# Exponentials of the wide attention taken by ScalarE straight from the scores, one operation per head and batch

## The chip, the cores and the metric

The kernel runs on one core of one Trainium2 chip. The metric is the device time of one execution in microseconds (us). A difference of 0.2%, some 2.3 us, is about what a measurement of this kernel can tell from none.

## The reference, cut to what matters

The program is a decoder layer stack over 64 batches of 64 tokens of width 128: attention with 16 narrow heads and a cross attention, a mixture of experts, attention with 16 heads of 64 and rotary embedding, a cross attention with a padding mask and a quantised feed-forward. The change lies in the second attention alone, after a layer norm of x:

```
q, k, v = x @ Wq, x @ Wk, x @ Wv          # 16 heads of 64
q, k = apply_rope(q), apply_rope(k)
sim = einsum('bid,bjd->bij', q, k) * scale  # scale = 64 ** -0.5
sim = where(causal, sim, -inf)
attn = softmax(sim, axis=-1)
out = einsum('bij,bjd->bid', attn, v)
x = x + out @ Wo + bo
```

All of it is computed in float32; the mask is added by a small bf16 matmul.

## The kernel before, in words

Phases follow one another: narrow attention, a plan, the experts, the wide attention (`wide_attention_phase`, names with the prefix a_ in the trace), and the tail. The wide attention takes 16 blocks of 4 batches (256 tokens). A block has G = 4 steps, and a step handles one item: 4 heads of these 4 batches. An item's scores fill `S_ps`, four banks of PSUM with 128 columns each in use (2 batches side by side, 2 one above the other), and there is one `S_ps` only.

Each engine has its own instruction stream, written out by hand and ordered by semaphores; `run_blocks_farther` gives a prologue, step(0), a loop and the last three blocks. In the step of item n the engines do, in this order:

- TensorE (PE): `scores(n+1)` (8 mask matmuls, L1552, and 64 small ones, L1560), `transpose_e(n)` (L1569), the projections `project_q(n+3)`, `project_v(n+1)`, `project_k(n+3)` (L1514, L1537, L1524), in a block's first step `transpose_x` of the next block (L1503), which borrows the first bank of `S_ps`, then `project_o(n-1)` (L1596) and `weigh_values(n)` (L1584).
- VectorE (DVE): `subtract_max(n+1)`: a row maximum (L1789) and the scores less that maximum written to `E` in SBUF (L1793), the semaphore `d_ready`; `products_q(n+3)` (L1765, two instructions); `reciprocals(n+1)`: row sums of `E` (L1799) and their reciprocals (L1804); `products_k(n+3)` (L1765, two); and by the step number g in the block: `combine` of the experts' rows (g = 0 and 1, L1737), `statistics` (g = 2, L1745 to L1752), `centres` (g = 3, L1759). In g = 1 `add_residual` (L1810) stands behind `subtract_max`. The last two blocks have none of combine, statistics and centres.
- ScalarE (ACT): `evacuate_e(n)` (L1681), `exponentials(n+1)` (L1674, one instruction on `E` in place, 128x512), `evacuate_v(n+1)` (L1670), `keep_xT` or `evacuate_xT` in two of the steps, `evacuate_o(n)` (L1688), and in g = 3 `normalise` (L1645), which waits for `centres`; `slots_of` (L1695) opens g = 0.
- GpSimd (POOL): `normalise_e(n+1)` (L1440, `E` times the reciprocals), the rotations of q and k of item n+3 (L1419, L1420), a gather of expert rows (L1456).

The waits that matter: `scores(n+1)` writes `S_ps` and so waits for `d_ready` of item n. `weigh_values(n)` waits for `v_ready` of item n+1, that is for `evacuate_v(n+1)`, which stands behind `exponentials(n+1)` in ScalarE's stream. `transpose_e(n)` waits for `normalise_e(n)` and for the products of k of item n+2, with which it shares a bank.

Of the kernel before, what the change touches and what calls it, by code (L numbers as in the profile page):

```python
# [7 lines left out]
P = 128  # L8
B, T, C = 64, 64, 128
# [10 lines left out]
ALU = mybir.AluOpType  # L20
ACT = mybir.ActivationFunctionType
AX = mybir.AxisListType
# [44 lines left out]
def wait_here(eng, sem, value, passed):  # L67

    eng.wait_ge(sem, value)
    eng.sem_inc(passed, 1)  # L70
# [1220 lines left out]
def wide_attention_phase(nc, k):  # L1291
    UB = 2
# [4 lines left out]
    G = H // 4  # L1297
    GH = 4
    ITEMS = NB * G
    SCALE = float(D1) ** -0.5  # L1300
    n = "a1"
    d = k.d
    with ExitStack() as ctx:
        def sb(name, shape, dt=F32):
            return ctx.enter_context(nc.sbuf_tensor(f"{n}_{name}", shape, dt))

        def ps(name, shape):
            return ctx.enter_context(nc.psum_tensor(f"{n}_{name}_ps", shape, F32))

        def sem(name):  # L1310
            return nc.alloc_semaphore(f"{n}_{name}")
# [26 lines left out]
        row_max = sb("row_max", [P, 2, GH * UB])  # L1338
        row_sum = sb("row_sum", [P, 2, GH * UB])
        rsum = sb("rsum", [P, 2, GH * UB])  # L1340

        E = sb("E", [P, 2, GH * P])
        ET = sb("ET", [P, 2, GH * P])
# [6 lines left out]
        S_ps = ps("S", [P, GH, 512])  # L1350
# [22 lines left out]
        v_ready = sem("v_ready")  # L1373
        s_ps = sem("s_ps")
        max_ready = sem("max_ready")
        d_ready = sem("d_ready")
        sum_ready = sem("sum_ready")
        e_ready = sem("e_ready")
        rsum_ready = sem("rsum_ready")
        en_ready = sem("en_ready")  # L1380
        et_ps = sem("et_ps")
# [5 lines left out]
        passed = sem("passed")  # L1387
# [4 lines left out]
        def item_at(blk, g):  # L1392

            return blk + g // G, g % G

        def later(number, least):

            return not isinstance(number, int) or number >= least

        def at_most_all(number):  # L1400

            return min(number, ITEMS) if isinstance(number, int) else number
# [93 lines left out]
        def _(pe):  # L1496
            def transpose_x(nb):

                pe.wait_ge(xn_ready, nb + 1)
                if later(nb, 1):  # L1500
                    pe.wait_ge(d_ready, nb * G - 2)
                for u in range(UB):
                    mm = nc.tensor.transpose(S_ps[:, 0, u * P:(u + 1) * P], xn[:, u, :], k.ident[:])  # L1503
                mm.then_inc(xnT_ps, 1)
# [35 lines left out]
            def scores(blk, g):  # L1540

                n_ = blk * G + g
                pe.wait_ge(rq_ready, n_ + 1)
                if later(n_, 1):
                    pe.wait_ge(d_ready, n_)
                if g == 2:
                    pe.wait_ge(xnT_ready, min(blk + 2, NB) if isinstance(blk, int) else blk + 2)
                wait_here(pe, rk_ready, n_ + 1, passed)
                for h in range(GH):
                    half = slice(64 * (h % 2), 64 * (h % 2) + 64)  # L1550
                    for b in range(2):
                        nc.tensor.matmul(S_ps[64 * b:64 * b + 64, h, 0:P], k.causal_queries[half, 0:T], k.causal_keys[half, 0:P],  # L1552
                                         start=True, stop=False)
                for a in range(2):
                    for u in range(UB):
                        for b in range(2):
                            tok = slice((2 * b + u) * T, (2 * b + u + 1) * T)
                            for h in range(GH):
                                rows = slice(32 * h, 32 * h + 32)
                                mm = nc.tensor.matmul(S_ps[64 * b:64 * b + 64, h, u * T:(u + 1) * T], RQ[rows, g % 2, a, tok],  # L1560
                                                      RK[rows, g % 2, a, tok], start=False, stop=(a == 1 and u == UB - 1))
                mm.then_inc(s_ps, 1)
# [9 lines left out]
            def weigh_values(blk, g):  # L1572

                n_ = blk * G + g
                pe.wait_ge(et_ready, n_ + 1)
                pe.wait_ge(v_ready, at_most_all(n_ + 2))
                wait_here(pe, pq_ready, at_most_all(n_ + 4), passed)
                for j in range(2):
                    for b in range(2):
                        for u in range(UB):  # L1580
                            rows = slice(64 * u, 64 * u + 64)
                            for r in range(2):
                                h = 2 * j + r
                                mm = nc.tensor.matmul(VQ_ps[64 * r:64 * r + 64, u, j * P + b * T:j * P + (b + 1) * T],  # L1584
                                                      V[rows, g % 2, b, h * D1:(h + 1) * D1],
                                                      ET[rows, g % 2, h * P + b * T:h * P + (b + 1) * T], start=True, stop=True)
                mm.then_inc(pv_ps, 1)

            def project_o(blk, g):
                n_ = blk * G + g  # L1590
                pe.wait_ge(ot_ready, n_ + 1)
                if g == 0 and later(blk, 1):
                    pe.wait_ge(x_done, blk)
                for u in range(UB):
                    for j in range(2):
                        mm = nc.tensor.matmul(Y_ps[:, u * P:(u + 1) * P], OT[:, g % 2, u, j, :], wo[:, g, j, :],  # L1596
                                              start=(g == 0 and u == 0 and j == 0),
                                              stop=(g == G - 1 and u == UB - 1 and j == 1), skip_group_check=True)
                mm.then_inc(y_ps, 1)
# [12 lines left out]
            def step(blk, prev, nxt):  # L1612
                for g in range(G):
                    if g + 1 < G or nxt:
                        scores(*item_at(blk, g + 1))
                    transpose_e(blk, g)
                    if g + 3 < G or nxt:
                        project_q(*item_at(blk, g + 3))
                    if g + 1 < G or nxt:
                        project_v(*item_at(blk, g + 1))  # L1620
                    if g + 3 < G or nxt:
                        project_k(*item_at(blk, g + 3))
                    if nxt and g == 0:
                        transpose_x(blk + 1)
                    if g > 0:
                        project_o(blk, g - 1)
                    elif prev:
                        project_o(blk - 1, G - 1)
                    weigh_values(blk, g)

            prologue()
            step(0, prev=False, nxt=True)
            with pe.Fori(1, NB - 1) as blk:
                step(blk, prev=True, nxt=True)
            step(NB - 1, prev=True, nxt=False)
            project_o(NB - 1, G - 1)

        @block.scalar
        def _(act):
# [30 lines left out]
                nc.scalar.activation(V[:, g % 2].rearrange("p b e -> p (b e)"), V_ps, ACT.Copy).then_inc(v_ready, 1)  # L1670

            def exponentials(blk, g):
                act.wait_ge(d_ready, blk * G + g + 1)
                nc.scalar.activation(E[:, g % 2, :], E[:, g % 2, :], ACT.Exp, scale=SCALE).then_inc(e_ready, 1)  # L1674

            def evacuate_e(blk, g):
                n_ = blk * G + g
# [51 lines left out]
        def _(dve):  # L1729
# [53 lines left out]
            def subtract_max(blk, g):  # L1783

                n_ = blk * G + g
                dve.wait_ge(s_ps, n_ + 1)
                src = S_ps[:, :, 0:P].rearrange("p h (u t) -> p h u t", t=T)
                top = row_max[:, g % 2, :].rearrange("p (h u) -> p h u", u=UB)
                nc.vector.tensor_reduce(top, src, AX.X, ALU.max).then_inc(max_ready, 1)  # L1789
                if later(n_, 2):  # L1790
                    dve.wait_ge(et_ps, n_ - 1)
                dve.wait_ge(max_ready, n_ + 1)
                nc.vector.tensor_tensor(E[:, g % 2, :].rearrange("p (h u t) -> p h u t", u=UB, t=T), src,  # L1793
                                        top.unsqueeze(3).broadcast_to([P, GH, UB, T]), ALU.subtract).then_inc(d_ready, 1)

            def reciprocals(blk, g):
                n_ = blk * G + g
                dve.wait_ge(e_ready, n_ + 1)
                nc.vector.tensor_reduce(row_sum[:, g % 2, :], E[:, g % 2, :].rearrange("p (j t) -> p j t", t=T), AX.X, ALU.add)\  # L1799
                    .then_inc(sum_ready, 1)  # L1800
                if later(n_, 2):
                    dve.wait_ge(en_ready, n_ - 1)
                dve.wait_ge(sum_ready, n_ + 1)
                nc.vector.reciprocal(rsum[:, g % 2, :], row_sum[:, g % 2, :]).then_inc(rsum_ready, 1)  # L1804

            def add_residual(blk):
# [866 lines left out]
```

## Time and profile before

| what | value |
|---|---|
| three timed runs | 1155.99, 1156.0, 1155.08 us; median 1155.99 us |
| the profiled execution's own time | 1161.69 us |
| its span | 1159.9 us |
| mean granted TensorE clock | 0.898 of full speed |
| busy: PE, DVE, ACT, POOL | 997.4, 845.9, 589.2, 564.1 us |
| 800 to 900 us (wide attention): PE, DVE, ACT, POOL | 97.19, 95.57, 43.86, 86.61 us |

The profile is of one execution. Busy times are per engine and overlap; matmuls are pipelined and their ends are modelled, so a busy PE is not a PE at its peak. The wide attention runs from about 606 to 1011 us of the span.

### The profile page before, as it was taken

The page shows a single profiled execution, that of the slowest core. Times are in us where ns is not written, and L with a number is a line of the kernel's source. Part 1 is how long each engine was busy: PE and PEld are TensorE (multiplying, and loading weights), DVE is VectorE, ACT ScalarE, POOL GpSimd, SP SyncE. Part 2 cuts the span into 40 slices and gives each one's busy share as a digit, 9 for nine tenths or more (in the row PEclk, how much of TensorE's full clock was granted, in tenths as well). Part 3 has the DMA queues.
Part 4 walks back from the last instruction along what each step waited for, and adds up shares of the span by engine and source line. Part 5 has one row for each costly group of instructions (what it writes and reads, how often), then busy time and mean ns, then how long its engine had stood idle before and what let it go on. Part 6 is the DMA issues. An engine that isn't in the chain of part 4 may idle for free. (4 is left out here: it accounts for less than half of the span.)

```text
span 1159.9 us, 38655 instructions
## 1 busy us (share of the span) xinstructions
PE 997.4 (86%) x14756; PEld 801.9 (69%) x14759; DVE 845.9 (73%) x2025; ACT 589.2 (51%) x983; POOL 564.1 (49%) x705
## 2 busy tenths in 40 slices
PE   5999999999945799999947999999999999776454
PEld 2666666667642799999936888888888888654113
DVE  4878787888749244444328999999999998488576
ACT  3665656677720466666612444444444444356545
POOL 4332424353300433333226888888888887433104
PEclk9999999999955799999978999999999999856555
DMA  7200000000000111111130000000000000050002
GB/s 240 114 2 0 2 11 20 20 19 27 11 28 0 40 47 48 48 48 47 39 109 13 13 12 11 11 11 9 11 11 11 11 7 1 17 127 24 1 0 73
DMA packets 36984, 37.60 MB, mean 32 GB/s; under 512 B 7142, under 2 KB 31145, under 8 KB 36522
## 3 DMA queue, kind: packets, MB, share of 16 engines
q1 hardware_dynamic: 31690, 27.33, 7.7%
q0 software_dynamic: 4352, 8.92, 3.0%
q8 instruction: 48, 0.79, 0.3%
q10 hardware_dynamic: 866, 0.33, 0.1%
q14 instruction: 28, 0.23, 0.1%
HBM read 27.65 MB, written 8.91 MB: 32 GB/s over the span
## 5 line engine op out<-in xcount | busy, mean ns | idle before, releaser
L1283 POOL DMA_INDIRECT e_x<-xn_rows,e_where x72 | 68.4, 950 | 167.2 <-DVE e_where L1264 119.4
L360 POOL TENSOR_SCALAR n_KX<-n_KT,n_of_head 128x512 f32<-128x512 f32 x124 | 84.1, 700 | 123.1 <-ACT n_KT L601 86.3
L1253 DVE COPY e_y<-e_Y_ps 128x128 f32<-128x128 f32 x72 | 21.0, 292 | 112.4 <-PE e_Y_ps L1220 105.9
L760 DVE TENSOR_REDUCE n_row_max<-n_S_ps 128x16 f32<-128x1024 f32 x64 | 78.2, 1221 | 28.2 <-PE n_S_ps L451 28.1
L1440 POOL TENSOR_TENSOR a_E<-a_E,a_rsum 128x512 f32<-128x512 f32 x64 | 66.7, 1042 | 56.0 <-DVE a_rsum L1804 56.0
L665 ACT ACTIVATE n_ET<-n_ET_ps 128x1024 f32<-128x1024 f32 x64 | 65.5, 1024 | 46.6 <-PE n_ET_ps L461 45.8
L461 PEld LDWEIGHTS n_ET_ps<-ident,n_E 128*128 128x128 f32 x512 | 57.1, 142 | 34.9 <-issue 20.1
L764 DVE TENSOR_TENSOR n_E<-n_S_ps,n_row_max 128x1024 f32<-128x1024 f32 x64 | 78.4, 1225 | 2.9
L1210 PE MATMUL e_G_ps<-e_xT,e_gate_here 128*128 128x128 f32 x576 | 78.5, 281 | 0.9 <-ACT e_up_here L1173 0.9
L1688 ACT ACTIVATE a_OT<-a_VQ_ps 128x512 f32<-128x512 f32 x64 | 38.2, 597 | 78.4 <-PE a_VQ_ps L1584 78.4
L1220 PE MATMUL e_Y_ps<-m_down_w,e_hT 128*128 x576 | 76.7, 275 | 1.1 <-issue 0.8
L1210 PE MATMUL e_U_ps<-e_xT,e_up_here 128*128 128x128 f32 x576 | 77.6, 279 | 0.0
L461 PE MATMUL n_ET_ps<-ident,n_E 128*128 128x128 f32 x512 | 68.3, 276 | 8.1 <-ACT n_E L657 8.1
L657 ACT ACTIVATE n_E<-n_E 128x1024 f32<-128x1024 f32 x64 | 67.2, 1052 | 14.2 <-DVE n_E L764 14.2
L1210 PEld LDWEIGHTS e_G_ps<-e_xT,e_gate_here 128*128 128x128 f32 x576 | 72.3, 197 | 1.1 <-ACT e_up_here L1173 1.1
L474 PEld LDWEIGHTS n_PV_ps<-n_VB,n_ET 128*64 128x64 f32 x2048 | 65.3, 138 | 10.5 <-issue 10.5
L1184 ACT ACTIVATE e_silu<-e_G_ps 128x512 f32<-128x512 f32 x72 | 43.0, 597 | 58.3 <-PE e_G_ps L1210 48.1
L1210 PEld LDWEIGHTS e_U_ps<-e_xT,e_up_here 128*128 128x128 f32 x576 | 71.7, 196 | 0.0
L474 PE MATMUL n_PV_ps<-n_VB,n_ET 128*64 128x18 f32 x2048 | 71.7, 213 | 0.0
L1220 PEld LDWEIGHTS e_Y_ps<-m_down_w,e_hT 128*128 128x128 f32 x576 | 70.2, 192 | 1.8 <-issue 1.8
L1674 ACT ACTIVATE a_E<-a_E 128x512 f32<-128x512 f32 x64 | 40.2, 629 | 61.1 <-DVE a_E L1793 61.1
L1596 PEld LDWEIGHTS a_Y_ps<-a_wo,a_OT 128*128 128x128 f32 x512 | 66.6, 193 | 4.7 <-ACT a_OT L1688 1.2
(278 smaller groups left out, 2672.4 us busy)
## 6 DMA issues: line engine op xcount, KB each, us to landing
slot_out<-e_y SPq DMA_DIRECT2D x72, 64.0 KB
X<-in_x SPq DMA_DIRECT2D x8, 256.0 KB, 5.8
n_ctxT<-in_ctxT SPq DMA_DIRECT2D x8, 256.0 KB, 3.0
m_gate_w<-in_L_ffn_gate_w SPq DMA_DIRECT2D x1, 2048.0 KB, 7.5
m_up_w<-in_L_ffn_up_w SPq DMA_DIRECT2D x1, 2048.0 KB, 11.9
m_down_w<-in_L_ffn_down_w SPq DMA_DIRECT2D x1, 2048.0 KB, 17.7
xn_rows<-n_xn SPq DMA_DIRECT2D x8, 256.0 KB
t_ctxT<-in_ctxT SPq DMA_DIRECT2D x8, 256.0 KB
```

The lines of the kernel that those rows point to most:

```text
L360: last = nc.gpsimd.tensor_scalar(KX[:, p, :, h * T:(h + 1) * T], src, of_head[:, h:h + 1], 1.0, ALU.mult, ALU.mult)
L461: mm = nc.tensor.transpose(ET_ps[:, j * P:(j + 1) * P], E[:, u % 2, j * P:(j + 1) * P], k.ident[:])
L474: mm = nc.tensor.matmul(PV_ps[64 * b:64 * b + 64, j * VW:(j + 1) * VW], ET[:, u % 2, j * P + b * T:j * P + (b + 1) * T], VB[:, p, (2 * u + ...
L657: nc.scalar.activation(E[:, u % 2, :], E[:, u % 2, :], ACT.Exp, scale=1.0 if is_cross(blk) else float(D0) ** -0.5).then_inc(e_ready, 1)
L665: nc.scalar.activation(ET[:, u % 2, :], ET_ps[:], ACT.Copy).then_inc(et_ready, 1)
L760: nc.vector.tensor_reduce(row_max[:, u % 2, :], src, AX.X, ALU.max).then_inc(max_done, 1)
L764: nc.vector.tensor_tensor(E[:, u % 2, :].rearrange("p (j t) -> p j t", t=T), src, row_max[:, u % 2, :].unsqueeze(2).broadcast_to([P, H, T] ...
L1210: mm = nc.tensor.matmul(out[:, c * P:(c + 1) * P], w[:, p, c * P:(c + 1) * P], xT[:, p, :], start=True, stop=True)
L1220: mm = nc.tensor.matmul(Y_ps[p][:, 0:C], hT[:, p, c * P:(c + 1) * P], down_w[:, bass.ds(e * F + c * C, C)], start=(c == 0), stop=(c == FC ...
L1283: nc.gpsimd.indirect_dma_start(out=x[:, j, :], out_offset=None, in_=k.xn_rows, in_offset=bass.IndirectOffsetOnAxis(ap=where[:, j, :], axis ...
L1440: nc.gpsimd.tensor_tensor(e, e, rsum[:, g % 2, :].unsqueeze(2).broadcast_to([P, GH * UB, T]), ALU.mult)\
L1596: mm = nc.tensor.matmul(Y_ps[:, u * P:(u + 1) * P], OT[:, g % 2, u, j, :], wo[:, g, j, :], start=(g == 0 and u == 0 and j == 0), stop=(g = ...
```

## The change

ScalarE now reads the scores in PSUM itself, with minus the scaled row maximum as bias, one operation per head and batch (a row of 128 partitions by 64 columns), and sums each row along the way. VectorE no longer subtracts the maximum and no longer sums the rows; it multiplies the 128x8 maxima by -SCALE into a new tile `low`. The scores' bank is free once the exponentials are done (`e_ready` takes the place of `d_ready` in `scores` and `transpose_x`), and `transpose_x` moves behind `project_o` in TensorE's order.

```diff
+        low = sb("low", [P, 2, GH * UB])
...
             def transpose_x(nb):
...
-                    pe.wait_ge(d_ready, nb * G - 2)
+                    pe.wait_ge(e_ready, nb * G - 2)
...
             def scores(blk, g):
...
-                    pe.wait_ge(d_ready, n_)
+                    pe.wait_ge(e_ready, n_)
...
-                    if nxt and g == 0:
-                        transpose_x(blk + 1)
                     if g > 0:
                         project_o(blk, g - 1)
                     elif prev:
                         project_o(blk - 1, G - 1)
+                    if nxt and g == 0:
+                        transpose_x(blk + 1)
                     weigh_values(blk, g)
...
             def exponentials(blk, g):
-                act.wait_ge(d_ready, blk * G + g + 1)
-                nc.scalar.activation(E[:, g % 2, :], E[:, g % 2, :], ACT.Exp, scale=SCALE).then_inc(e_ready, 1)
+                n_ = blk * G + g
+                act.wait_ge(max_ready, n_ * 2 + 2)
+                if later(n_, 2):
+                    act.wait_ge(et_ps, n_ - 1)
+                    act.wait_ge(rsum_ready, n_ - 1)
+                for h in range(GH):
+                    for u in range(UB):
+                        j = h * UB + u
+                        last = nc.scalar.activation(E[:, g % 2, j * T:(j + 1) * T], S_ps[:, h, u * T:(u + 1) * T], ACT.Exp,
+                                                    bias=low[:, g % 2, j:j + 1], scale=SCALE,
+                                                    accum_out=row_sum[:, g % 2, j:j + 1])
+                last.then_inc(e_ready, 1)
...
                 nc.vector.tensor_reduce(top, src, AX.X, ALU.max).then_inc(max_ready, 1)
                 if later(n_, 2):
-                    dve.wait_ge(et_ps, n_ - 1)
-                dve.wait_ge(max_ready, n_ + 1)
-                nc.vector.tensor_tensor(E[:, g % 2, :].rearrange("p (h u t) -> p h u t", u=UB, t=T), src,
-                                        top.unsqueeze(3).broadcast_to([P, GH, UB, T]), ALU.subtract).then_inc(d_ready, 1)
+                    dve.wait_ge(e_ready, n_ - 1)
+                wait_here(dve, max_ready, n_ * 2 + 1, passed)
+                nc.vector.tensor_scalar(low[:, g % 2, :], row_max[:, g % 2, :], -SCALE, None, ALU.mult).then_inc(max_ready, 1)
...
                 dve.wait_ge(e_ready, n_ + 1)
-                nc.vector.tensor_reduce(row_sum[:, g % 2, :], E[:, g % 2, :].rearrange("p (j t) -> p j t", t=T), AX.X, ALU.add)\
-                    .then_inc(sum_ready, 1)
                 if later(n_, 2):
                     dve.wait_ge(en_ready, n_ - 1)
-                dve.wait_ge(sum_ready, n_ + 1)
                 nc.vector.reciprocal(rsum[:, g % 2, :], row_sum[:, g % 2, :]).then_inc(rsum_ready, 1)
```

## Rows read from the trace of the kernel before

**Rows 1.** The page, part 1: busy time, share of the span, instructions of each engine.

```profile
PE 997.4 (86%) x14756; PEld 801.9 (69%) x14759; DVE 845.9 (73%) x2025; ACT 589.2 (51%) x983; POOL 564.1 (49%) x705
```

**Rows 2.** Stretches: length; PE, PEld, DVE, ACT, POOL busy; PE clock, DMA share, GB/s.

```profile
800.00:900.00 100.00, 97.19 (x2178) 85.15 (x2177) 95.57 (x179) 43.86 (x87) 86.61 (x109) 1.00 0.04 11
...
180.00:210.00 30.00, 27.43 (x400) 18.60 (x398) 23.92 (x55) 18.33 (x23) 12.42 (x16) 1.00 0.07 20
...
1000.00:1005.00 5.00, 3.96 (x20) 3.54 (x21) 2.27 (x4) 1.82 (x3) 0.32 (x1) 0.66 0.00 0
```

**Rows 3.** Timeline (start us, us, instruction, [idle before]): the same matmuls, one block apart.

```profile
801.28 0.69 PE L1584 MATMUL a_VQ_ps<-a_ET,a_V 64*64 64x64 f32 x32
...
825.28 0.69 PE L1584 MATMUL a_VQ_ps<-a_ET,a_V 64*64 64x64 f32 x32
```

**Rows 4.** Timeline, VectorE in a step with combine.

```profile
806.33 0.68 DVE L1799 TENSOR_REDUCE a_row_sum<-a_E 128x8 f32<-128x512 f32 x1
...
807.11 0.20 DVE L1804 RECIPROCAL a_rsum<-a_row_sum 128x8 f32<-128x8 f32 x1
...
808.42 1.59 DVE L1737 SCALAR_TENSOR_TENSOR X<-a_expert_rows,gates,X 128x128 f32 x2
...
809.93 0.68 DVE L1789 TENSOR_REDUCE a_row_max<-a_S_ps 128x8 f32<-128x512 f32 x1
...
810.72 0.69 DVE L1793 TENSOR_TENSOR a_E<-a_S_ps,a_row_max 128x512 f32<-128x512 f32 x1
...
811.33 0.68 DVE L1765 TENSOR_TENSOR a_PQ<-a_VQ_ps,a_cos 128x512 f32<-128x512 f32 x1
```

**Rows 5.** Timeline, VectorE in the steps with statistics and with centres.

```profile
814.61 0.47 DVE L1745 BATCH_NORM_STATS2 a_stats<-X 128x6 f32 x2
...
815.94 0.68 DVE L1789 TENSOR_REDUCE a_row_max<-a_S_ps 128x8 f32<-128x512 f32 x1
...
820.62 0.72 DVE L1759 SCALAR_TENSOR_TENSOR a_centre<-a_mv,a_rstd 128x2 f32<-128x2 f32 x1
```

**Rows 6.** Timeline, TensorE and ScalarE in the step of rows 4.

```profile
806.93 0.69 PE L1584 MATMUL a_VQ_ps<-a_ET,a_V 64*64 64x64 f32 x32
...
807.39 0.18 PEld L1552 LDWEIGHTS a_S_ps<-causal_keys,causal_queries 64*64 64x64 bf16 x8
...
808.58 0.63 PE L1569 MATMUL a_KE_ps<-ident,a_E 128*128 128x128 f32 x4
...
809.25 0.60 ACT L1681 ACTIVATE a_ET<-a_KE_ps 128x512 f32<-128x512 f32 x1 [0.96 <-PE a_KE_ps L1569]
...
811.45 0.63 ACT L1674 ACTIVATE a_E<-a_E 128x512 f32<-128x512 f32 x1 [1.60 <-DVE a_E L1793]
...
811.98 0.58 ACT L1670 ACTIVATE a_V<-a_VQ_ps 128x512 f32<-128x512 f32 x1
```

**Rows 7.** Groups by form: busy us, mean ns | idle before; ScalarE, and a small VectorE one.

```profile
L652 ACT ACTIVATE m_LG<-n_G_ps 128x32 f32<-128x32 f32 x6 | 1.2, 198 | 3.7 <-PE n_G_ps L502 3.7
...
L601 ACT ACTIVATE n_KT<-n_G_ps 128x512 f32<-128x512 f32 x8 | 4.8, 597 | 3.9 <-PE n_G_ps L412 3.4
...
L599 ACT ACTIVATE n_KT<-n_G_ps,n_bk 128x512 f32<-128x512 f32 x8 | 5.5, 687 | 2.4 <-PE n_G_ps L412 2.1
...
L2346 DVE TENSOR_SCALAR t_var_eps<-t_mv 128x4 f32<-128x4 f32 x16 | 3.0, 189 | 0.5
```

**Rows 8.** Timeline, ScalarE instructions behind one another.

```profile
821.54 0.88 ACT L1645 ACTIVATE a_xn<-X,a_centre,a_rstd 128x128 f32 x2 [1.27 <-DVE a_centre L1759]
...
822.32 0.19 ACT L1695 ACTIVATE a_where<-slots 128x4 int32 x1
...
822.42 0.57 ACT L1681 ACTIVATE a_ET<-a_KE_ps 128x512 f32<-128x512 f32 x1
...
822.90 0.62 ACT L1674 ACTIVATE a_E<-a_E 128x512 f32<-128x512 f32 x1
```

**Rows 9.** Timeline, TensorE's scores matmuls near the end, no combine left on VectorE.

```profile
987.22 0.31 PE L1552 MATMUL a_S_ps<-causal_keys,causal_queries 64*64 64x128 bf16 x8
...
992.89 0.29 PE L1552 MATMUL a_S_ps<-causal_keys,causal_queries 64*64 64x128 bf16 x8
```

More of the change, by code:

```diff
@@ L1375, in wide_attention_phase @@
         max_ready = sem("max_ready")
-        d_ready = sem("d_ready")
-        sum_ready = sem("sum_ready")
         e_ready = sem("e_ready")
```

## The prediction

> **What bounds the kernel now.** I read the busy shares of the page first, then the stretch table over the wide attention, then its timeline instruction by instruction. Over the span TensorE leads with 86% [rows 1]. In the stretch that the change touches two engines are full: from 800 to 900 us TensorE is busy 97.19 and VectorE 95.57 of 100 us, ScalarE only 43.86, and the TensorE clock is 1.00 [rows 2]. The reader is to see there that work taken from VectorE and given to ScalarE looks free by the shares.
>
> A block of four items takes 825.28 - 801.28 = 24.00 us [rows 3], 6.00 per item. Near the end, in the blocks without combine, statistics and centres on VectorE, an item takes 992.89 - 987.22 = 5.67 us [rows 9]. So VectorE sets the 6.00 and TensorE's own floor is about 5.67, with the next block's row transposes (0.2 us) some 22.9 us per block. That is the most that relief of VectorE can bring: 1.1 us a block.
>
> **What the change takes from VectorE.** In an item the subtraction holds its stream for 811.33 - 810.72 = 0.61 us and the row sums for 807.11 - 806.33 = 0.78 [rows 4]. The new 128x8 multiply costs about 0.19 by the nearest small operation (128x4, 189 ns [rows 7]) and waits for the maximum as the subtraction did. VectorE is down by about 1.2 of its 6.0 us per item. It is then no longer full, so what counts is latency.
>
> **What it adds to ScalarE.** One exponential of 128x512 held ScalarE's stream for 811.98 - 811.45 = 0.53 us [rows 6]. Eight of 128x64 take its place. A plain copy out of PSUM takes 198 ns at 32 columns and 597 at 512, so 0.83 ns per column and 0.225 us at 64; a pointer bias adds 687 - 597 = 0.090 [rows 7]. That is 0.315 us each. The two pointer-scaled instructions of 0.486 us take 0.88 together and the next instruction starts 0.78 after the first [rows 8]: instructions overlap by 0.09, pointers included. Start to start, an exponential costs 0.315 - 0.09 = 0.225 us.
>
> The row sum has no row in this trace. Its lower end is nothing (a sum can't shorten the operation): start to start x = 0.225 us. If the accumulator is read out by a small instruction of its own, the nearest row is the 128x4 activate, which holds the stream for 822.42 - 822.32 = 0.10 us [rows 8]: x = 0.325. If the read waits until the exponential has drained and nothing overlaps, x = 0.315 + 0.19 = 0.50, the upper end. I take 0.325, since a result per row has to be written to another tile than the exponentials. The eight then last 8x + 0.09 = 2.69 us from first start to last end.
>
> The page "VectorE: DVE Perf Modes" of the Trainium skill (section on two Vector instructions with no wait between them) says that on VectorE an operation that also writes its accumulator is two instructions, the main one and a read. It says nothing of ScalarE, and no row here shows either.
>
> **Two loops that the exponentials now close.** Let E be the end of exponentials(n+1), and a hand-over between engines 0.05 us (transposes end 808.58 + 0.63, the evacuation starts 809.25: 0.04; the subtraction ends 811.41, the exponential starts 811.45 [rows 4, 6]).
>
> Loop A, through TensorE: evacuate_v starts at E - 0.09 and takes 0.58, so V is there at E + 0.49; weigh_values at E + 0.54; scores 0.46 behind it (806.93 to 807.39, where their weight loads begin), at E + 1.00; evacuate_e 1.86 behind the scores' start (809.25 - 807.39), at E + 2.86 [rows 6]; it holds ScalarE 0.48 (822.90 - 822.42) [rows 8], so the next exponentials can start at E + 3.34. Period: 3.43 + 8x. Before, 8x was 0.53 and this loop had over 2 us to spare; no other edit hides it, since weigh_values(n) stands in order before scores(n+2).
>
> Loop B, through VectorE: the reciprocal now waits for E, and products_k, combine and the next maximum are queued behind it. Reciprocal at E + 0.05; combine 808.42 - 807.11 = 1.31 later; the maximum 809.93 - 808.42 = 1.51 later; the multiply 0.79 behind the maximum's start [rows 4]; 0.19 for itself and 0.05: exponentials at E + 3.90, a period of 3.99 + 8x. In the statistics step 1.33 stands for 1.51 (815.94 - 814.61 [rows 5]): 3.81 + 8x. In the centres step VectorE is through at E + 0.05 + 1.31 + 0.72 = E + 2.08 [rows 5], before the scores end, so loop A decides, and the normalise (0.78) and slots (0.10) pair that waits for the centre starts at 2.13 and puts the evacuation at E + 3.01: 3.58 + 8x. The products of q (1.2 us) and in one step the residual (0.4) lie under the exponentials.
>
> Block: 2 x 3.99 + 3.81 + 3.58 + 32x = 15.4 + 32x. It equals 24.0 at x = 0.27. At x = 0.325 it is 25.8, or 1.8 us more per block.
>
> **The moved transposes.** transpose_x waits for the exponentials of the item of its step, at E + 0.05, takes 0.4, and lies before weigh_values at E + 0.54, which waits anyway; its evacuation ends by about E + 0.85, under scores at E + 1.00. Cost nothing, up to 0.2 us a block if this is tight. Left where it was, it would have held project_o too. Both ends: 0 and 3 us in all. POOL is later by as much as E and has slack: normalise_e ends near E + 1.4 and transpose_e wants it at E + 2.2.
>
> **The sum.** 14 blocks with VectorE's extra work: 14 x 1.8 = 25 us. The last two blocks: 7 items from 5.67 to 3.43 + 2.6 = 6.03, 2.5 us. First and last item, exposed: maximum to reciprocals grows from 0.79 + 0.69 + 0.05 + 0.63 + 0.05 + 0.78 to 0.79 + 0.19 + 0.05 + 2.69 + 0.05, 0.8 each, 1.6. Together +29 us: 1161.69 to 1191 for an execution like the profiled one, and 1156 to 1185 for the median, since the profiled one was 5.7 us above it.
>
> **Rivals.**
>
> Faster, the row sum free (x = 0.225): the block would be 15.4 + 7.2 = 22.6, below TensorE's floor of 22.9, so 1.1 us less in 14 blocks, 15 us less: 1141. For it: TensorE and VectorE are the full engines and ScalarE is half idle [rows 2]. Against it: sums must leave the engine by some write. It decides below x = 0.27, so if the sum costs under 0.045 us. The page "ScalarE: Activation LUTs" of the Trainium skill (What ACT_TABLE_LOAD costs) gives 280 ns + 0.833 per column with a pointer bias and 93 ns of overlap, 0.24 us here, and names an accumulator output without a price: read so, an estimate from that page is 15.4 + 7.7 = 23.1 a block and 1143 or so. The trace agrees on all that the page prices.
>
> Slower by much, the read-out drains the engine (x = 0.50): 31.4 a block, 14 x 7.4 = 103, the last seven items 12, the ends 3: 1274. For it: a read must follow the last element. Against it: ScalarE's other instructions overlap without regard to what they are [rows 8].
>
> The clock falls: TensorE waits some 0.8 us per item where it hardly waited. For it: 1000 to 1005 us, with long waits, shows 0.66 [rows 2]. Against it: 180 to 210 us had 27.43 of 30 us busy at 1.00 [rows 2], and I forecast about 5.67 of 6.4. At half clock the 5.67 us of TensorE would near 10, over 200 us in all. It can only come with x near 0.5.
>
> **How the numbers follow.** Forecast case (x from 0.275 to 0.40, 1159 to 1225): 0.50, at 1185. Sum (nearly) free: 0.22 faster. The gap between (x about 0.27, within 0.2%): 0.05. Read-out that drains wholly or in part (x over 0.40): 0.20. Clock: 0.03. The range leaves out the lowest few microseconds of the free case and the drained end: 1144 to 1245, which is x up to 0.44. Within the forecast case alone 1165 to 1215. Faster 0.22, same 0.05, slower 0.73.
>
> **What would show it.** Right: L1674 with 8 operations an item near 0.315 us, a second kind of instruction beside them or starts 0.3 us or more apart; the reciprocal directly behind the last exponential; the maximum late behind combine, with ScalarE idle before L1674 on VectorE in two or three steps of four; weigh_values waiting for a_V; blocks of 25 to 26 us; TensorE's clock still 1.00. Wrong: exponentials 0.23 us apart and blocks of 23 us with TensorE dense, or 0.5 apart and blocks over 30.

## The result and the profile after

The changed kernel takes 1201.36 us (median of 4 runs, 1200.75 to 1202.81) against 1155.99 us before: ratio 1.039, 95% interval 1.0372 to 1.0407. The forecast was 1185, slower, range 1144 to 1245.

The page of the changed kernel, part 1, answers to [rows 1]; the stretch 800 to 900 us, with the columns of [rows 2], stands under it:

```profile
PE 996.9 (83%) x14756; PEld 804.2 (67%) x14759; DVE 789.3 (66%) x1961; ACT 706.5 (59%) x1943; POOL 563.0 (47%) x705
```
```profile
800.00:900.00 100.00, 86.80 (x1924) 76.75 (x1924) 72.63 (x147) 67.68 (x302) 77.58 (x98) 1.00 0.04 10
```

No engine is full any more, and TensorE's clock is still 1.00. TensorE's busy time over the span has not changed (996.9 against 997.4 us): the 39 us that the span has grown (1159.9 to 1198.9 us) are waits. Who waits, 740 to 940 us, some 30 steps (total us, times, longest):

```profile
DVE a_rsum L1809 <- ACT a_E L1680: 36.6, 30, 1.5
...
PE a_VQ_ps L1583 <- ACT a_V L1669: 25.9, 30, 1.0
...
ACT a_E L1680 <- DVE a_low L1802: 13.1, 23, 0.6
```

In 30 of 30 steps the reciprocal waits for the exponentials and weigh_values for V, and in 23 ScalarE waits for `low`. The page's groups for the exponentials:

```profile
L1680 ACT ACTIVATE a_E<-a_S_ps,a_low 128x64 f32<-128x64 f32 x512 | 152.3, 324 | 33.4 <-DVE a_low L1802 32.0
...
L1680 ACT ACTIVATION_READ_ACCUMULATOR a_E<-a_S_ps,a_low 128x1 f32 x512 | 110.9, 217 | 0.0
```

Each row sum is a second instruction of 217 ns. What follows is one loop in the timeline, from a step's exponentials to the next ones:

```profile
805.02 0.31 ACT L1680 ACTIVATE a_E<-a_S_ps,a_low 128x64 f32<-128x64 f32 x1 [0.59 <-DVE a_low L1802]
...
805.23 0.19 ACT L1680 ACTIVATION_READ_ACCUMULATOR a_E<-a_S_ps,a_low 128x1 f32 x1
805.33 0.30 ACT L1680 ACTIVATE a_E<-a_S_ps,a_low 128x64 f32<-128x64 f32 x1
...
807.26 0.24 ACT L1680 ACTIVATION_READ_ACCUMULATOR a_E<-a_S_ps,a_low 128x1 f32 x1
807.35 0.63 ACT L1669 ACTIVATE a_V<-a_VQ_ps 128x512 f32<-128x512 f32 x1
807.53 0.20 DVE L1809 RECIPROCAL a_rsum<-a_row_sum 128x8 f32<-128x8 f32 x1 [1.48 <-ACT a_E L1680]
...
808.30 0.59 PEld L1583 LDWEIGHTS a_VQ_ps<-a_ET,a_V 64*64 64x64 f32 x32 [1.20 <-issue]
...
809.13 0.17 PEld L1551 LDWEIGHTS a_S_ps<-causal_keys,causal_queries 64*64 64x64 bf16 x8 [0.25 <-issue]
...
810.35 0.69 DVE L1798 TENSOR_REDUCE a_row_max<-a_S_ps 128x8 f32<-128x512 f32 x1 [1.39 <-PE a_S_ps L1559]
...
810.89 0.72 POOL L1419 TENSOR_TENSOR a_RK<-a_PK 128x256 f32<-128x256 f32 x1
811.01 0.60 ACT L1690 ACTIVATE a_ET<-a_KE_ps 128x512 f32<-128x512 f32 x1 [0.48 <-PE a_KE_ps L1568]
811.19 0.45 DVE L1802 TENSOR_SCALAR a_low<-a_row_max 128x8 f32<-128x8 f32 x1
...
811.68 0.31 ACT L1680 ACTIVATE a_E<-a_S_ps,a_low 128x64 f32<-128x64 f32 x1
```

The eight exponentials and sums last from 805.02 to 807.50, 2.48 us, and 4.18 us later the next ones start. The surprise is in the rows of GpSimd and of `low`: the multiply that makes `low` starts at 811.19 and ends at 811.64, 0.03 us behind GpSimd's rotation (810.89 + 0.72). A step with combine ahead shows the same:

```profile
815.47 1.61 DVE L1746 SCALAR_TENSOR_TENSOR X<-a_expert_rows,gates,X 128x128 f32 x2
...
816.16 0.77 POOL L1419 TENSOR_TENSOR a_RQ<-a_PQ 128x256 f32<-128x256 f32 x1
...
816.90 0.77 POOL L1418 TENSOR_TENSOR a_RK<-a_PK 128x256 f32<-128x256 f32 x1
...
817.00 0.68 DVE L1798 TENSOR_REDUCE a_row_max<-a_S_ps 128x8 f32<-128x512 f32 x1
...
817.63 0.72 POOL L1419 TENSOR_TENSOR a_RK<-a_PK 128x256 f32<-128x256 f32 x1
817.84 0.54 DVE L1802 TENSOR_SCALAR a_low<-a_row_max 128x8 f32<-128x8 f32 x1 [0.15 <-DVE a_row_max L1798]
...
818.41 0.31 ACT L1680 ACTIVATE a_E<-a_S_ps,a_low 128x64 f32<-128x64 f32 x1 [0.56 <-DVE a_low L1802]
```

817.84 + 0.54 = 818.38 and 817.63 + 0.72 = 818.35: 0.03 again. By the timeline 58 of the 64 multiplies end 0.03 to 0.04 us behind a rotation of k; the other six take 0.17 us. The page "SBUF — State Buffer" of the Trainium skill (section on who interferes with whom) has a mechanism for it: a VectorE instruction in a two-port mode and a GpSimd instruction share a pair of ports, and the one that comes second is blocked until the first has ended. The ends in the trace agree with that; that this multiply runs in such a mode no row shows, and the runs low_psum below test whether GpSimd is what holds it. I call it the lock.

### The profile page after: what moved, and what is told of

Read it like the earlier page. It is cut to its first block and busy times, and to the rows that moved or that the text cites. A ratio compares the mean times of both kernels' runs of the same rounds, so it can differ in the third digit from the quotient of the medians.

```text
span 1198.9 us, 39717 instructions
## 1 busy us (share of the span) xinstructions
PE 996.9 (83%) x14756; PEld 804.2 (67%) x14759; DVE 789.3 (66%) x1961; ACT 706.5 (59%) x1943; POOL 563.0 (47%) x705
## 5 line engine op out<-in xcount | busy, mean ns | idle before, releaser
L1680 ACT ACTIVATE a_E<-a_S_ps,a_low 128x64 f32<-128x64 f32 x512 | 152.3, 324 | 33.4 <-DVE a_low L1802 32.0
L1680 ACT ACTIVATION_READ_ACCUMULATOR a_E<-a_S_ps,a_low 128x1 f32 x512 | 110.9, 217 | 0.0
L1583 PE MATMUL a_VQ_ps<-a_ET,a_V 64*64 64x64 f32 x2048 | 44.5, 223 | 49.0 <-ACT a_V L1669 43.0
L1583 PEld LDWEIGHTS a_VQ_ps<-a_ET,a_V 64*64 64x64 f32 x2048 | 37.5, 134 | 60.0 <-issue 59.8
L1172 ACT ACTIVATE e_gate_here<-m_gate_w 128x512 f32 x72 | 45.3, 629 | 46.1 <-PE e_U_ps L1210 23.4
L1690 ACT ACTIVATE a_ET<-a_KE_ps 128x512 f32<-128x512 f32 x64 | 38.2, 597 | 57.2 <-PE a_KE_ps L1568 57.2
```

The costliest lines, as they stand in the source:

```text
L1680: last = nc.scalar.activation(E[:, g % 2, j * T:(j + 1) * T], S_ps[:, h, u * T:(u + 1) * T], ACT.Exp, bias=low[:, g % 2, j:j + 1], scale=S ...
```

## Experiments

For each kernel the block is the mean distance of evacuate_o four items apart, read from the timeline between 690 and 945 us. The kernel before was run on the same chip each time; its median there was 1156 to 1162 us, so ratios are compared.

| kernel | ratio to before, 95% interval | block, us |
|---|---|---|
| before | 1 | 24.12 |
| changed | 1.039 (1.0372 to 1.0407) | 26.88 |
| t_move_only | 0.9976 (0.996 to 0.9992) | 24.09 |
| t_old_place | 1.0369 (1.0347 to 1.0392) | 26.88 |
| no_sums | 0.9973 (0.996 to 0.9986) | 23.98 |
| one_exp | 0.9939 (0.9914 to 0.9964) | 23.52 |
| combine_first | 1.0351 (1.0326 to 1.0375) | 26.66 |
| v_middle | 1.0438 (1.041 to 1.0465) | 27.72 |
| low_psum | 1.0211 (1.0178 to 1.0244) | 25.56 |
| low_psum_comb | 1.0125 (1.0092 to 1.0158) | 24.90 |
| low_psum_both | 1.0017 (1.0002 to 1.0031) | 24.09 |
| sub_kept | 1.0196 (1.0165 to 1.0227) | 25.43 |
| sub_kept_v | 1.0255 (1.0223 to 1.0288) | 26.01 |
| sub_kept_both | 0.9901 (0.9872 to 0.993) | 23.19 |

**The moved transposes.** t_move_only is the kernel before, t_old_place the changed one, each with the other's order:

```diff
-                    if nxt and g == 0:
-                        transpose_x(blk + 1)
                     ... project_o ...
+                    if nxt and g == 0:
+                        transpose_x(blk + 1)
```

> The kernel before with nothing but transpose_x moved behind project_o. The two-loop theory: no cost, 1156 us within 0.2%, since VectorE is full and sets the block of 24.0 us. Rival, that the move itself is part of the loss (evacuation of the transposes late under the next scores): up to 0.4 us in each of 15 blocks, 1159 to 1162.

> The changed kernel with transpose_x back ahead of project_o. It then waits for the exponentials and holds project_o (0.9 us) and weigh_values behind it. The two-loop theory: weigh_values comes at E + 1.3 and not at E + 0.8 in one step of four, 0.5 us more a block, 15 blocks, so 1209 against 1201. Rival, that TensorE's place does not matter because VectorE's loop (reciprocal, products, combine, maximum) decides in that step: 1201 to 1203.

Neither moves the block. In the kernel before the move costs nothing, as expected (if anything, 0.2% gained). In the changed kernel the old place makes one step 7.14 us and the next 6.24, where the changed kernel has 6.65 and 6.73: the loss of 0.5 us is there, and it is given back one step later, which I had not counted. The move is not part of the result.

**The price of the sums and of the split.** no_sums leaves out the row sums (the reciprocals are taken of the maxima), and its edit stands first; one_exp takes a single exponential of 128x512 without bias and sums. Neither computes the attention; they are there for their times:

```diff
-                                                    bias=low[:, g % 2, j:j + 1], scale=SCALE,
-                                                    accum_out=row_sum[:, g % 2, j:j + 1])
+                                                    bias=low[:, g % 2, j:j + 1], scale=SCALE)
```
```diff
-                for h in range(GH):
-                    for u in range(UB):
...
+                last = nc.scalar.activation(E[:, g % 2, :].rearrange("p (h t) -> p h t", h=GH), S_ps[:, :, 0:P], ACT.Exp, scale=SCALE)
```

> The changed kernel without the row sums (the reciprocals are taken of the maxima instead, so the normalisation is left out of the result). It prices the accumulator: the two-loop theory says that the exponentials go from 0.291 to about 0.225 us start to start, 0.55 us off each item's exponentials, 2.2 us off each of 14 blocks and 0.5 off the last eight items: 1201 - 35 = 1166. Rival, that the exponentials' length is covered by other work and only the later maximum (combine ahead of it) costs: under 5 us gained, 1196 or more.

Without the accumulators the whole loss is gone: ratio 0.9973 and block 23.98, some 48 us gained where 35 were expected. (The loss is not theirs alone: the runs below take it away by other edits, with the sums in place.) The timeline of no_sums merges the eight of a step into one row:

```profile
811.12 1.75 ACT L1680 ACTIVATE a_E<-a_S_ps,a_low 128x64 f32<-128x64 f32 x8 [0.26 <-DVE a_low L1801]
```

1.75 us against 2.48: 0.73 less per item, and 4 x 0.73 = 2.9 us a block, which is what it moved (26.88 - 23.98 = 2.90). From the end of one item's exponentials to the start of the next nothing has changed: 4.26, 4.26, 4.29 and 4.18 us in the four steps, in both kernels. The rival, under 5 us in all, falls. An exponential is (1.75 - 0.33) / 7 = 0.20 us apart without its sum and 0.29 with it ((807.06 - 805.02) / 7 in the changed kernel, by its timeline): a sum costs 0.09 us. I had expected 0.225 without it, hence the larger gain.

> The changed kernel with one exponential of 128x512 from the scores in place of eight, without bias and sums (so the maximum is not subtracted and the rows are not normalised by their sums); low is still computed and waited for. It prices the split itself: with no_sums, blocks were 23.98 us. One operation of 0.6 us in place of eight of 1.75 takes 1.2 us more from each loop, which then lies under TensorE's own order: blocks of 23.0 to 23.3 us, ratio 0.987 to 0.99. Rival, that the multiply behind GpSimd's lock or something else still decides: blocks of 24.

Block 23.52, ratio 0.994: 0.46 us a block less than no_sums, not 4 x 1.2, since TensorE's order is reached (98.57 of 100 us busy); the ratio is less good than the 0.987 to 0.99 expected, since two steps of four still take 6.2 and 6.0.

**VectorE's queue.** combine_first moves combine, statistics and centres ahead of the reciprocals:

```diff
+                    (combine, statistics or centres of step g)
                     reciprocals(*item_at(blk, g + 1))
                     products_k(*item_at(blk, g + 3))
-                    (combine, statistics or centres of step g)
```

> The changed kernel with combine, statistics and centres ahead of the reciprocals in VectorE's order, so that they fill the wait for the exponentials. The two-loop theory: loop B is opened; the loop that is left goes over a_V, weigh_values, scores, maximum and low, E + 3.8 and not E + 4.26 or 4.29 in three steps of four, 1.35 us less a block, 14 blocks: 1201 - 19 = 1182. Rival, that TensorE's wait for a_V alone sets the time (loop A): no change, 1199 to 1203.

Neither: ratio 1.035, 0.2 us a block and not 1.35. Its timeline shows why:

```profile
807.80 0.69 DVE L1798 TENSOR_REDUCE a_row_max<-a_S_ps 128x8 f32<-128x512 f32 x1 [1.12 <-PE a_S_ps L1559]
...
808.65 0.75 DVE L1802 TENSOR_SCALAR a_low<-a_row_max 128x8 f32<-128x8 f32 x1 [0.15 <-DVE a_row_max L1798]
808.65 0.73 POOL L1419 TENSOR_TENSOR a_RK<-a_PK 128x256 f32<-128x256 f32 x1
...
809.57 0.31 ACT L1680 ACTIVATE a_E<-a_S_ps,a_low 128x64 f32<-128x64 f32 x1 [0.59 <-DVE a_low L1802]
```

The maximum now waits for the scores, so combine is out of the loop, but the 128x8 multiply takes 0.75 us and ends with GpSimd's last rotation. That rotation stands a fixed way behind the exponentials: reciprocal, normalise_e, four rotations, which end 4.06 us behind the reciprocal's start. It is a third loop, through GpSimd, and in the changed kernel it was already the longest: there the rotations end 4.06 to 4.16 us behind the reciprocal's start and the multiply 0.03 behind them, while VectorE's own loop, as low_psum will show, wants 3.9. The 0.2 us that combine_first gains are in the same rows: with combine beside them two rotations take 0.77 us, as at 816.16 and 816.90 above, and the last one ends 0.10 us later in two steps of four; moved, combine no longer meets them.

**The lock.** low_psum puts the maxima into a free corner of the last scores bank, so that the multiply reads PSUM:

```diff
-                top = row_max[:, g % 2, :].rearrange("p (h u) -> p h u", u=UB)
+                maxima = S_ps[:, GH - 1, 256:256 + GH * UB]
+                top = maxima.rearrange("p (h u) -> p h u", u=UB)
...
-                nc.vector.tensor_scalar(low[:, g % 2, :], row_max[:, g % 2, :], -SCALE, ...
+                nc.vector.tensor_scalar(low[:, g % 2, :], maxima, -SCALE, ...
```

> The changed kernel with the row maxima in an unused part of the last scores bank, so that the multiply that makes low reads PSUM and not SBUF. The lock theory: in the changed kernel the multiply (171 ns at its shortest, 542 at the median) starts and then ends 0.03 us behind GpSimd's rotation, each time; read from PSUM it takes 0.2 and the exponentials start 0.35 us earlier in each step, about 1.3 us off a block of 26.9, 18 us in all: ratio to before 1.024 instead of 1.039. Rival, that a 128x8 operation behind a dependent reduction simply takes 0.5 us (pipeline, semaphores): no change, ratio 1.037 or more.

The multiply in the changed kernel and in low_psum (shortest, median, longest in ns, first and last start):

```profile
L1802 DVE TENSOR_SCALAR a_low<-a_row_max x64: 171/542/774, 616.0 to 1040.7; 128x8 f32<-128x8 f32 x64
```
```profile
L1803 DVE TENSOR_SCALAR a_low<-a_S_ps x64: 165/167/169, 615.1 to 1019.1; 128x8 f32<-128x8 f32 x64
```

From up to 774 ns to 169 at most, with the place of the maxima the only change, and 1.32 us off the block (1.3 expected; ratio 1.021, 1.024 expected). The rival (a dependent small operation simply takes 0.5 us) falls. Nor is PSUM merely the faster source: from SBUF the multiply takes 171 ns where no rotation holds it up.

> The same with combine, statistics and centres ahead of the reciprocals. The lock theory: with combine alone moved, the loop went over reciprocal, normalise_e and four rotations on GpSimd to the end of the multiply (E + 4.1), which is why it gained only some 0.4%. Without the lock the loop is a_V, weigh_values, scores, maximum, multiply: E + 3.6, against 4.26, 4.29 and 4.18: 2.2 to 2.6 us off each of 14 blocks, 31 to 36 us: ratio 1.009 to 1.013. Rival, that combine was never in the loop and the two edits only give what low_psum gives alone: ratio 1.024.

1.0125 and 24.90: with the lock gone the same move of combine gains 0.66 us a block where it had gained 0.22. Both together give 1.98 us a block (26.88 - 24.90), 0.2 to 0.6 short of what was expected. What is left is loop A, through TensorE. In low_psum_comb the exponentials before these rows end at 808.59:

```profile
808.43 0.64 ACT L1669 ACTIVATE a_V<-a_VQ_ps 128x512 f32<-128x512 f32 x1
...
809.38 0.59 PEld L1583 LDWEIGHTS a_VQ_ps<-a_ET,a_V 64*64 64x64 f32 x32 [0.50 <-issue]
...
809.85 0.21 PEld L1551 LDWEIGHTS a_S_ps<-causal_keys,causal_queries 64*64 64x64 bf16 x8
...
811.69 0.60 ACT L1690 ACTIVATE a_ET<-a_KE_ps 128x512 f32<-128x512 f32 x1 [0.92 <-PE a_KE_ps L1568]
...
812.18 0.31 ACT L1680 ACTIVATE a_E<-a_S_ps,a_low 128x64 f32<-128x64 f32 x1
```

The exponentials start at E + 3.59, directly behind evacuate_e, where the prediction's loop A had E + 3.34: V ends at 809.07 and weigh_values comes 0.31 us later, not 0.05. In three steps of four the exponentials of this run stand so behind evacuate_e.

**Where V is evacuated.** In these the loop over the heads has one more line:

```diff
                 for h in range(GH):
+                    if h == 2:
+                        evacuate_v(blk, g)
                     for u in range(UB):
```

> The changed kernel with evacuate_v between the fourth and the fifth exponential and nothing else. The loops through the end of the exponentials (reciprocal, then VectorE's queue and GpSimd's rotations up to the multiply's end) say that it gets slower: the exponentials end 0.5 us later in each item and nothing that they release was bound by a_V, 2 us more a block: 28.9 us, ratio 1.06. Rival, that TensorE's wait for a_V (1.0 us an item in the changed kernel's waits) is what costs: that wait goes, block near 24, ratio 1.00.

Slower than the changed kernel, 27.72 us a block, though TensorE's wait for a_V, the longest that TensorE has, is more than halved (11.0 us from 25.9 in the same stretch). Its place is taken by the next wait, for `low`:

```profile
ACT a_E L1680 <- DVE a_low L1802: 13.1, 23, 0.6
```
```profile
ACT a_E L1682 <- DVE a_low L1801: 25.5, 21, 1.5
```

(first the changed kernel, then v_middle). The direction is as expected, the size 0.84 us a block and not 2. With V among them the exponentials last 0.50 us longer in each item, and in three steps of four the way from their end to the next ones is as long as before (4.26, 4.26, 4.29); in the fourth, with centres, it falls from 4.18 to 3.03: 4 x 0.50 less 1.15 is 0.85.

> The same again with evacuate_v between the fourth and the fifth exponential of its item, so that weigh_values does not wait for the last one. The two-loop theory: scores then wait for the exponentials directly (E + 0.3), the next exponentials start at E + 2.7 and last 3.0 with the evacuation among them: 5.7 us an item, which is TensorE's own 5.67. Blocks of 22.9 to 23.3 us against 24.0 before: ratio 0.986 to 0.991. Rival, that ScalarE's longer row of instructions costs as much as the wait did: as low_psum_comb, 1.01 or more.

24.09: level with before, and the 0.986 to 0.991 not reached. TensorE is 97.74 of 100 us busy, and two steps take 5.7 and 5.8, but the step with transpose_x takes 6.6. There the transposes wait 0.3 us for the end of the exponentials and stand ahead of weigh_values and the scores. No run moved them here, so that they cost the 1 us is read and not shown.

**The subtraction kept on VectorE.** Only the sums move to ScalarE:

```diff
-                nc.scalar.activation(E[:, g % 2, :], E[:, g % 2, :], ACT.Exp, scale=SCALE).then_inc(e_ready, 1)
+                for h in range(GH):
+                    for u in range(UB):
+                        j = h * UB + u
+                        last = nc.scalar.activation(E[...j...], E[...j...], ACT.Exp, scale=SCALE,
+                                                    accum_out=row_sum[:, g % 2, j:j + 1])
+                last.then_inc(e_ready, 1)
```

> The kernel before with only the row sums moved to ScalarE (eight exponentials in SBUF, 0.24 us apart), all orders as before. By the loop over VectorE (maximum 0.79, subtraction 0.69, exponentials 2.15, reciprocal and products 1.35, combine 1.5 or statistics 1.3): 6.5 and 6.3 us in three steps of four, 6.0 in the fourth: blocks of 25.3 us, ratio 1.01 to 1.02, slower although VectorE has 0.8 us less to do an item. Rival, busy time decides: VectorE is relieved, TensorE's 23.2, ratio 0.99.

> The same with evacuate_v between the fourth and the fifth exponential, combine still behind the products of k. The loop over VectorE gets 0.5 us longer: 7.1, 7.1, 6.9 and 5.8 us, blocks of 26.9, ratio 1.03, against 23.2 and 0.990 with combine ahead of the reciprocals as well. Rival, that evacuate_v's place brings the gain and combine's place little: ratio 0.99.

> The kernel before with only the row sums moved to ScalarE: VectorE still subtracts the maximum into E and frees the scores' bank at once, ScalarE takes eight exponentials in SBUF with a sum each, evacuate_v stands between the fourth and the fifth, combine ahead of the reciprocals. VectorE loses 0.78 us an item and no loop goes through the exponentials. Two-loop theory: TensorE's floor, 5.67 an item, 22.9 a block, 14 x 1.1 = 15 us off before: ratio 0.987. Rival, that TensorE's floor is not reached since the exponentials in SBUF hold up evacuate_e or GpSimd's normalisation: ratio 0.995 to 1.01.

sub_kept: 25.43 (25.3 expected). It is slower than before although VectorE does less and the scores' bank is freed early: the loop needs neither the bank nor `low`, the reciprocal's wait in VectorE's queue suffices. In sub_kept the reciprocal waits, and combine and the maximum follow in order with no wait of their own:

```profile
809.81 0.20 DVE L1808 RECIPROCAL a_rsum<-a_row_sum 128x8 f32<-128x8 f32 x1 [0.75 <-ACT a_E L1679]
...
811.10 1.61 DVE L1744 SCALAR_TENSOR_TENSOR X<-a_expert_rows,gates,X 128x128 f32 x2
...
812.63 0.68 DVE L1796 TENSOR_REDUCE a_row_max<-a_S_ps 128x8 f32<-128x512 f32 x1
```

sub_kept_v is slower still, 26.01 (26.9 expected). Both orders together give 23.19 and ratio 0.990 (0.987 expected), the one version that computes the attention and is faster than before by clearly more than 0.2%: 1144.99 us beside 1156.46. Its stretch 800 to 900 us has TensorE at 99.33:

```profile
800.00:900.00 100.00, 99.33 (x2195) 88.50 (x2194) 78.88 (x170) 70.35 (x356) 89.30 (x114) 1.00 0.04 11
```

V's early evacuation costs 0.6 us a block where combine stands in VectorE's loop (25.43 to 26.01). With combine out of it no run of this pair varied V alone; between low_psum_comb and low_psum_both the same edit gains 0.8 us.

## Why the prediction was right, and what it missed

**Right.** VectorE set the 24.0 us and TensorE's floor was near 23: sub_kept_both stops at 23.19 (three steps of 5.65 and one, with the transposes, of 6.24, so these cost 0.6 us and not 0.2). VectorE's loop was right to a hundredth where nothing hides it: 3.90 forecast, 3.89 in low_psum's steps with combine. The read-out is an instruction of its own that overlaps (0.09 us, forecast 0.10), so the free case and the drained case fall. The exponentials close loops that had slack; TensorE idles in every step; the clock stays at 1.00; the moved transposes cost nothing.

**The sum.** Per block the forecast was 25.8, measured 26.88. Four items' exponentials: 4 x 2.69 forecast, 4 x 2.48 measured, 0.8 less, since an exponential without its sum is 0.20 us apart and not 0.225. From their end to the next start: 3.90, 3.90, 3.72 and 3.49 forecast (the periods less 8x and 0.09), 4.26, 4.26, 4.29 and 4.18 measured in the four steps of one block, 2.0 more. Net 1.1 to 1.2 us in 14 blocks, 16 us, which is the gap between 1185 and 1201. So two errors of opposite sign partly cancel, and that the gap is no larger is luck: 29 us of loss were forecast and 45 came. (In the drained case the two ends come to 4.4 us by the same working and not 3, which changes nothing.)

**The mis-sized term** is "0.19 for itself", the multiply that makes `low`. It takes 0.45 to 0.63 us in that block, since GpSimd is rotating; low_psum shows that this is worth 1.32 us a block and 1.8% of the time. The trace of before had the sign of it. The 128x2 operation of centres takes 0.72 us there [rows 5], and ends 0.02 behind a rotation:

```profile
820.60 0.72 POOL L1419 TENSOR_TENSOR a_RQ<-a_PQ 128x256 f32<-128x256 f32 x1
```

In the changed kernel it takes 0.15, where it starts just as one GpSimd instruction gives way to the next (808.81, with the rotation from 808.82). I took the small operation from the tail phase [rows 7], where 15 of the 16 took 0.17 us with GpSimd idle, and put the centre's 0.72 into the sum without asking why.

**A second, smaller one** is the hand-over of 0.05 us. Towards a TensorE that really waits it is 0.32: V ends at 807.98 and the weight loads start at 808.30. Loop A was so 0.27 us too short, and in the centres step, where the way over V and the scores is nearly as long as GpSimd's (it still takes 3.98 to 4.06 us in low_psum, without the lock), that and 0.37 us more between weigh_values and scores (808.30 to 809.13 against 0.46) make up most of the difference (3.49 to 4.18). In the statistics step 0.13 us more lie between the end of the multiply and the exponentials (0.17, and 0.03 in the others). No run varied any of the three.

**What I had not seen at all** is the third loop, through GpSimd's queue and the lock. The prediction says that GpSimd "has slack" and looks only at normalise_e; the four rotations behind it end 4.1 to 4.2 us after the exponentials, and as the multiply ends behind them, theirs is the loop that set the changed kernel's steps, 0.37 us longer than loop B in the steps with combine (4.26 against 3.89). The forecast had VectorE's queue as the loop that decides; that holds for low_psum and not for the changed kernel. Without the lock combine_first would have gained what loop B said, 1.35 us; low_psum_comb against low_psum shows half of that, because loop A, with TensorE's longer hand-over, takes over. The price of an exponential was off too, and in the rivals as well: without its sum it is 0.20 us from the next one, not 0.225 or the 0.24 of the estimate in the rival "Faster". Nor did the trace of before agree on all that the page "ScalarE: Activation LUTs" of the Trainium skill (What ACT_TABLE_LOAD costs) prices, as that rival says: the page's figures make 0.24 us of what the rows made 0.225.

## What to carry to other kernels

Before work goes to a half-idle engine, write down the loop that it closes: what must end before it starts, what stands in order behind it on each engine, and how long until it can start again; busy shares say nothing of that. A wait put at the wrong place in a full queue (reciprocals ahead of combine) costs more than the instructions that the change saves, and the longest wait in the table is not the one to remove: the loop with the largest sum is. And take the price of a small SBUF-to-SBUF VectorE operation from a place where GpSimd is as busy as it will be; where GpSimd's work hangs on the same event, it closes a loop of its own.

## What the runs showed of the hardware

A 128x8 VectorE multiply from SBUF to SBUF took 171 to 774 ns and in 58 of 64 cases ended 0.03 to 0.04 us behind a GpSimd tensor_tensor (changed kernel); read from PSUM it took 165 to 169 ns (low_psum). Reductions and tensor_tensor operations of 128x512 that read PSUM kept their 0.65 to 0.69 us beside the same rotations. The other way round, GpSimd rotations beside combine took 0.77 us and not 0.72.

The sum of an activate is a separate 128x1 instruction on ScalarE, 217 ns on average in the changed kernel and 187 in sub_kept, that overlaps its neighbours and adds 0.09 us (no_sums). Start to start, a 128x64 exponential with its sum took 0.29 us from PSUM with a pointer bias and 0.24 from SBUF without one (sub_kept).

Between the end of ScalarE's V and the weight loads that wait for it lay 0.31 to 0.32 us, between ScalarE's exponentials and VectorE's reciprocal 0.03 (changed kernel and low_psum_comb).
